# Chunked gated slot attention with a quantised SwiGLU on one core: two transposes taken from TensorE, its loop written out

## The reference

```
n = layernorm(x)
q, k, v, g, s = n@Wq, n@Wk, n@Wv, n@Wg, clip(n@Ws, -32, 32)     # 16 heads; q,k,s 64 wide, v,g 128 wide
z = cumlogsumexp(s, time);  p_t = exp(s_t - z_t);  decay_t = exp(z_(t-1) - z_t)
hk_t = hk_(t-1)*decay_t + k_t (x) p_t ;  ok_t = q_t . hk_t      # 64 slots
w = softmax(ok over slots)
hv_t = hv_(t-1)*decay_t + p_t (x) v_t ;  o_t = w_t . hv_t
x = x + (rmsnorm(o)*g_norm * silu(g)) @ Wo
n = layernorm(x)
x = x + ((silu(n@fp8(gate_w)*gs) * (n@fp8(up_w)*us)) @ fp8(down_w)) * ds
```

## Time and profile before

| | us |
|---|---|
| median of 3 runs | 1432.31 (1431.65 to 1432.43) |
| the profiled execution, whole | 1433.31 |
| its span, first to last instruction | 1431.2 |
| PE busy in the span | 1407.7 (98%) |
| DVE busy | 1001.8 (70%) |
| ACT busy | 430.1 (30%) |
| DMA packets, all queues | 63178, 57.23 MB |

### The profile page before, as it was taken

One profiled execution on the slowest core, in us unless ns is written; L12 is line 12 of the kernel. 1 busy time (PEld: TensorE's weight loads), 2 busy tenths in 40 slices (PEclk: granted clock), 3 DMA queues, 4 the chain that ended last, 5 costly groups with the idle time before them and its releaser, 6 DMA issues.

```text
span 1431.2 us, 23618 instructions
## 1 busy us (share of the span) xinstructions
PE 1407.7 (98%) x8480; PEld 1165.8 (81%) x8480; DVE 1001.8 (70%) x1619; ACT 430.1 (30%) x1243; POOL 144.1 (10%) x106
## 2 busy tenths in 40 slices
PE   7899999999999999999999999999999999999998
PEld 5788888888888888888888888888888878888886
DVE  8677777777777777777777777777777785535354
ACT  4223332333233323332333233323233323222221
POOL 3001110111011101110111011101110010000000
PEclk9999999999999999999999999999999999999999
DMA  6011001100110021002101110111010330000000
GB/s 177 17 56 41 20 26 56 41 19 27 56 41 19 29 61 43 19 27 62 44 19 37 45 41 19 49 40 34 19 54 1 118 118 0 30 0 29 0 30 30
DMA packets 63178, 57.23 MB, mean 40 GB/s; under 512 B 7408, under 2 KB 54256, under 8 KB 63088
## 3 DMA queue, kind: packets, MB, share of 16 engines
q1 hardware_dynamic: 63088, 55.87, 12.8%
HBM read 42.22 MB, written 13.63 MB: 39 GB/s over the span
## 4 chain that ended last, share of the span: by engine, by line
PE 95%; DVE 3%; DMA 1%; issue 0%; SPq 0%; POOL 0%; ACT 0%; DVEq 0%
PE bank L345 18%; PE bank L347 18%; PE bank L346 18%; PE bank L114 12%; PE bank L1384 6%; PE bank L533 4%; PE bank L466 3%; PE bank L516 2%; PE bank L416 2%; PE bank L408 2%; PE bank L455 2%; PE bank L521 1%; PE bank L482 1%; PE bank L438 1%; PE bank L494 1%; PE bank L503 1%
## 5 line engine op out<-in xcount | busy, mean ns | idle before, releaser
L345 PE MATMUL bank<-wvg_hi,xT_hi 128*128 128x512 f32 x512 | 209.0, 408 | 0.6 <-ACT a_and_v L596 0.6
L347 PE MATMUL bank<-wvg_hi,xT_lo 128*128 128x512 f32 x512 | 200.4, 391 | 0.0
L346 PE MATMUL bank<-wvg_lo,xT_hi 128*128 128x512 f32 x512 | 199.9, 390 | 0.0
L596 ACT ACTIVATE a_and_v<-bank 128x256 f32<-128x256 f32 x128 | 49.1, 383 | 296.1 <-PE bank L347 296.0
L954 DVE TENSOR_TENSOR y<-y,bank 128x512 f32<-128x512 f32 x128 | 87.6, 685 | 60.5 <-PE bank L347 60.4
L823 POOL TENSOR_TENSOR rstd<-ssq,neg_half 128x8 f32<-128x8 f32 x32 | 52.4, 1636 | 617.7 <-DVE ssq L925 617.7
L345 PEld LDWEIGHTS bank<-wvg_hi,xT_hi 128*128 128x128 f32 x512 | 96.3, 188 | 22.4 <-ACT a_and_v L596 1.0
L347 PEld LDWEIGHTS bank<-wvg_hi,xT_lo 128*128 128x128 f32 x512 | 96.1, 188 | 21.0
L346 PEld LDWEIGHTS bank<-wvg_lo,xT_hi 128*128 128x128 f32 x512 | 96.5, 188 | 17.3
L873 DVE RECIPROCAL cT<-cT 128x512 f32<-128x512 f32 x32 | 107.3, 3353 | 1.1
L345 PE MATMUL bank<-wo_hi,oT_hi 128*128 128x512 f32 x256 | 106.3, 415 | 0.0
(11 more groups left out here) (157 smaller groups left out, 3194.5 us busy)
## 6 DMA issues: line engine op xcount, KB each, us to landing
fp_weights<-q SPq DMA_DIRECT2D x28, 318.0 KB, 2.7
stage_vg<-in_L_attn_Wv SPq DMA_DIRECT2D x32, 128.0 KB, 2.8
stage_vg<-in_L_attn_Wg SPq DMA_DIRECT2D x32, 128.0 KB, 3.4
stage<-in_L_attn_Wo SPq DMA_DIRECT2D x16, 256.0 KB, 2.6
out<-n_then_result SPq DMA_DIRECT2D x16, 256.0 KB, 2.1
y<-in_L_attn_hidden_states SPq DMA_DIRECT2D x3, 1024.0 KB, 8.7
q<-in_L_ffn_gate_w SPq DMA_DIRECT2D x28, 106.0 KB, 2.0
q<-in_L_ffn_up_w SPq DMA_DIRECT2D x28, 106.0 KB, 2.2
```

The costliest lines, as they stand in the source:

```text
L345: pe.matmul(dst, w_hi, m_hi, start=(k == 0), stop=False)
L346: pe.matmul(dst, w_hi, m_lo, start=False, stop=False)
L347: last = pe.matmul(dst, w_lo, m_hi, start=False, stop=(k == n - 1))
L596: return act.activation(dst, src, ACT.Copy)
```

## The change

- For units 1 to 31 the seven transposes on TensorE and the two copies on ScalarE are gone. VectorE turns 32x32 blocks of `eT` and of the first 3 chunks of `kT` (`e_turn`, `k_turn`) into the tile `o`, which is free at that time. SP stores these in 4 DMAs each (`store_e`, `store_k`) to DRAM with the blocks put in their places, in pieces of 32 floats (128 bytes), and loads each back in 4 DMAs (`load_e`, `load_k`) of 32 partitions each, with rows of 2048 and 1536 bytes. This is done one unit ahead. Unit 0 keeps the transposes.
- TensorE's units 1 to 28 are written out; there is no loop left there in attention.
- `mean_square(u)` moves to the end of unit u, between the last two gates, and `out_norm` stands ahead of `clip`.
- The quantisation has 6 steps: the square, the test against the largest value and two scalings are replaced with one product that overflows and one sum.
- Ahead of unit 0, `sums(0, 0)` (L870, L873) is moved behind the masks of the scores and a gate.

```diff
+BK = 32
+BL = P // BK
-Q8_STEPS = 8
+Q8_STEPS = 6
+    e_blocks = o[:, 0, :, :].rearrange("p c d -> p (c d)")
+    k_blocks = o[:, 1, :, :].rearrange("p c d -> p (c d)")[:, 0:(CH - 1) * P]
...
+        def store_e(nu):
+            sp.wait_ge(s_eb, nu)
+            for i in range(BL):
+                sp.dma_start(e_dram.rearrange("t b (c i m) -> i t (b c) m", i=BL, m=BK)[i],
+                             e_blocks[BK * i:BK * (i + 1), :].rearrange("t (n m) -> t n m", m=BK)
+                             ).then_inc(s_est, 16)
+        def load_e(nu):
+            sp.wait_ge(s_est, 16 * BL * nu)
+            if isinstance(nu, int) and nu == 1:
+                sp.wait_ge(s_hvd, nu)
+            for b in range(BL):
+                sp.dma_start(e_tok[BK * b:BK * (b + 1), :, :].rearrange("t c m -> t (c m)"), e_dram[:, b, :]
+                             ).then_inc(s_eld, 16)
+        def store_k(nu):
+            sp.wait_ge(s_kb, nu)
...
+        def load_k(nu):
+            sp.wait_ge(s_oi, nu)
...
+        store_e(1)
+        load_e(1)
+        store_k(1)
         load_o(0, 1)
+        load_k(1)
         store_q8(0)
         with sp.Fori(0, PAIRS - 1) as h:
             for i in range(1, B + 1):
-                load_q8(h * B + i)
+                u = h * B + i
+                load_q8(u)
                 if i == 1:
                     load_skq(h + 1, 0)
                     load_vg(h + 1)
+                store_e(u + 1)
+                load_e(u + 1)
                 if i == 2:
                     load_skq(h + 1, 1)
+                store_k(u + 1)
+                if i == 2:
                     load_skq(h + 1, 2)
                     load_o(h + 1, 0)
                 if i == B:
                     load_o(h + 1, 1)
+                load_k(u + 1)
                 store_q8(h * B + i)
...
@@ TensorE, unit
-            pe.wait_ge(s_am, 2 * u + 1)
-            for c in range(CH - 1):
-                mm = pe.transpose(T0[:, c * P:(c + 1) * P], kT[:, c * P:(c + 1) * P], ident[:, :])
-            mm.then_inc(s_trk, 1)
-            pe.wait_ge(s_e, u + 1)
-            pe.wait_ge(s_am, 2 * u + 2)
-            for c in range(CH):
-                mm = pe.transpose(T1[:, c * P:(c + 1) * P], eT[par][:, c * P:(c + 1) * P], ident[:, :])
-            mm.then_inc(s_tre, 1)
+            if first:
...
-            if not first:
+            if first:
+                pe.wait_ge(s_ktok, 1)
+                pe.wait_ge(s_etok, 1)
+            else:
+                pe.wait_ge(s_kld, 16 * BL * u)
+                pe.wait_ge(s_eld, 16 * BL * u)
                 pe.wait_ge(s_oev, 2 * u)
...
+            if not first:
+                pe.wait_ge(s_am, 2 * u + 2)
             pe.wait_ge(s_v, (u + 1) * CH)
...
-        with pe.Fori(0, PAIRS - 1) as h:
-            pair_reg[0] = h
-            for i in range(1, B + 1):
-                unit(h * B + i, i)
+        for u in range(1, (PAIRS - 1) * B + 1):
+            unit(u, (u - 1) % B + 1)
@@ ScalarE, head_squares and unit
+            if not a and not last:
+                act.wait_ge(s_est, 16 * BL * (u + 1))
...
-            copy(k_tok.rearrange("p c k -> p (c k)"), T0[:, 0:(CH - 1) * P]).then_inc(s_ktok, 1)
...
-            copy(e_tok[:, :, :].rearrange("p c m -> p (c m)"), T1[:, :]).then_inc(s_etok, 1)
+            if first:
+                act.wait_ge(s_trk, 1)
+                copy(k_tok.rearrange("p c k -> p (c k)"), T0[:, 0:(CH - 1) * P]).then_inc(s_ktok, 1)
+                act.wait_ge(s_tre, 1)
+                copy(e_tok[:, :, :].rearrange("p c m -> p (c m)"), T1[:, :]).then_inc(s_etok, 1)
@@ VectorE
+        def e_turn(nu, ni):
+            dve.wait_ge(s_e, nu + 1)
+            if not (isinstance(nu, int) and nu == 1):
+                dve.wait_ge(s_tro, 2 * (nu - 1))
+            dve.transpose(e_blocks.rearrange("p (b c m) -> p b c m", b=BL, m=BK),
+                          eT[ni % 2][:, :].rearrange("p (c b t) -> p b c t", c=CH, t=BK)).then_inc(s_eb, 1)
+        def k_turn(nu):
+            dve.wait_ge(s_k, nu + 1)
+            dve.transpose(k_blocks.rearrange("p (b c m) -> p b c m", b=BL, m=BK),
+                          kT[:, 0:(CH - 1) * P].rearrange("p (c b t) -> p b c t", c=CH - 1, t=BK)
+                          ).then_inc(s_kb, 1)
...
-                lambda: dve.tensor_tensor(t, w, w, ALU.mult),
-                lambda: dve.tensor_scalar(t, t, FP8_MAX ** 2, FP8_MAX ** 2, ALU.max, ALU.subtract),
-                lambda: dve.tensor_scalar(t, t, HUGE, HUGE, ALU.mult, ALU.mult),
-                lambda: dve.scalar_tensor_tensor(out=w, in0=t, scalar=0.0, in1=w, op0=ALU.mult, op1=ALU.add))
+                lambda: dve.tensor_scalar(t, w, TO_INF, 0.0, ALU.mult, ALU.mult),
+                lambda: dve.tensor_tensor(w, w, t, ALU.add))
...
             if not first:
-                mean_square(u - 1)
-            if not last:
-                clip(nu, ni)
-            if not first:
                 out_norm(u - 1)
+            if not last:
+                clip(nu, ni)
             key_states(u)
             value_states(u)
             if not first:
                 out_lo(u - 1, A)
+            if not last:
+                e_turn(nu, ni)
...
                 add_y(u - 1, i - 1, 0)
                 add_y(u - 1, i - 1, 1)
+            if not last:
+                k_turn(nu)
...
             if not first:
                 dve.wait_ge(s_oi, u)
+            if not last:
+                dve.wait_ge(s_kst, 16 * BL * (u + 1))
             dve.tensor_tensor(wT[:, :], T1[:, :], cT[i % 2][:, :], ALU.mult).then_inc(s_wT, 1)
...
                 gate(2, nu, ni)
+                mean_square(u)
                 gate(3, nu, ni)
...
-        sums(0, 0)
         dve.wait_ge(s_const, 4)
         mask_scores(0, 0)
         gate(B - 1, 0, 0)
+        sums(0, 0)
```

More of the change, by code:

```diff
@@ L309, in store_q8 @@
                          q8[:, :, 0:n]).then_inc(s_fp8_out, 16)
+        def store_e(nu):
[13 more added lines that the diff above has]
+            sp.wait_ge(s_kb, nu)
+            for i in range(BL):
+                sp.dma_start(k_dram.rearrange("t b (c i m) -> i t (b c) m", i=BL, m=BK)[i],
+                             k_blocks[BK * i:BK * (i + 1), :].rearrange("t (n m) -> t n m", m=BK)
+                             ).then_inc(s_kst, 16)
+        def load_k(nu):
+            sp.wait_ge(s_oi, nu)
+            for b in range(BL):
+                sp.dma_start(k_tok[BK * b:BK * (b + 1), :, :].rearrange("t c m -> t (c m)"), k_dram[:, b, :]
+                             ).then_inc(s_kld, 16)
+        ffn.moves = (store_e, load_e, store_k, load_k)
         load_skq(0, 0)
@@ L350, in pair_of @@
         def pair_of(u, i):
-            return u // B if isinstance(u, int) else pair_reg[0] + i // B
-        pair_reg = [None]
+            return u // B
         def wait_drained(j, u):
@@ L383, in job @@
                     pe.wait_ge(s_vgl2, 2 * pair_of(u, i) + 2)
-            if j == ST and (not isinstance(u, int) or u < B):
+            if j == ST and u < B:
                 pe.wait_ge(s_xl, CH * (b + 1))
@@ L401, in scores @@
             pe.wait_ge(s_q, u + 1)
-            if not (isinstance(u, int) and u == 0):
+            if u:
                 pe.wait_ge(s_sub, u)
@@ L429, in unit @@
             nu, ni = u + 1, i + 1
[L431 to L439 removed]
+            if first:
+                pe.wait_ge(s_am, 1)
+                for c in range(CH - 1):
+                    mm = pe.transpose(T0[:, c * P:(c + 1) * P], kT[:, c * P:(c + 1) * P], ident[:, :])
+                mm.then_inc(s_trk, 1)
+                pe.wait_ge(s_e, 1)
+                pe.wait_ge(s_am, 2)
+                for c in range(CH):
+                    mm = pe.transpose(T1[:, c * P:(c + 1) * P], eT[par][:, c * P:(c + 1) * P], ident[:, :])
+                mm.then_inc(s_tre, 1)
             if not last:
@@ L632, in evac @@
             elif j == KTJ:
-                if not first:
-                    act.wait_ge(s_trk, u)
+                if isinstance(u, int) and u == 1:
+                    act.wait_ge(s_trk, 1)
+                elif not first:
+                    act.wait_ge(s_a, u)
+                    act.wait_ge(s_kb, u - 1)
                 copy(kT[:, :], src[:, :]).then_inc(s_k, 1)
@@ L721, in unit @@
                 evac(VG1, nu, ni)
-            head_squares(u, 0)
+            head_squares(u, 0, last)
             if tail and not last:
@@ L726, in unit @@
                 evac(VG2, nu, ni)
-            head_squares(u, 1)
+            head_squares(u, 1, last)
             if not last:
@@ L1326, in _ @@
         load_down(1)
+        store_e, load_e, store_k, load_k = ffn.moves
+        store_e(UNITS - 2)
+        load_e(UNITS - 2)
+        store_k(UNITS - 2)
+        load_k(UNITS - 2)
+        store_e(UNITS - 1)
+        load_e(UNITS - 1)
+        store_k(UNITS - 1)
         sp.wait_ge(w["projected"], JOBS * (UNITS - 1) + STEADY_JOBS.index(QT) + 1)
         load_gate_up(0)
+        load_k(UNITS - 1)
         sp.wait_ge(w["projected"], JOBS * UNITS)
```

33 lines of the change are left out of this document (15 added, 18 removed).

## The result

| | before | after |
|---|---|---|
| median of 6 runs each, us | 1432.37 (1431.63 to 1433.3) | 1409.46 (1407.86 to 1409.88) |
| profiled execution, us | 1433.31 | 1409.40 |
| its span, us | 1431.2 | 1407.3 |

A forecast was written before the change was run, and what follows sets the result against it. PE's instruction stream was taken as the bound (busy 98%). Terms -23.7 - 1.0 - 4.9 + 1.9 + 1.4 = -26.3 took the profiled 1433.3 to 1407.0, a median of 1406.0 us; range 1402 to 1424, 1402 to 1409 without rivals.

The forecast's parts named there:

- The transposes: PE, units 1 to 31: removing seven transposes per unit gains 0.77 us in 29 units, 0.68 in two, 23.7 in all.
- The loop: PE, units 1 to 29: writing out the loop's turns gains 1.0 us (0 to 1.0).
- The start of unit 0: Unit 0: with the sums behind the masks, L455 starts at 47.9 instead of 52.79, gaining 4.9 us.
- rival 3: Unit 0: the clock falls at 44 anyway or its stop lowers it; 3 to 5 us lost; chance 0.15.
- The stop in unit 0: Unit 0, L516: PE stands still waiting on k's store and L1059, losing 1.9 us (0 to 4).
- Wk behind the loads of e: Seven units with i = 2: Wk's later load uses up the exponential's slack before L503; 0.2 us each, 1.4 in all.
- The mark I had set, that ACT must not wait past offset 17: Sign against the forecast: ACT waiting for Wk later than 17 us after its unit begins.
- The price of small pieces: DMA of e and k: 15 ns per 128-byte packet, four stores taking 4.05 us from first issue to last landing.
- rival 1: DMA stores of e and k: small pieces cost as much as 512 bytes, 18 us more, 1424; chance 0.14.
- The mark of 5 us for the stores of e: Sign against the forecast: stores of e taking over 5 us from the first issue.
- Work on DVE: DVE: two new turns per unit at 0.7 us each, against two fewer quantisation passes net; DVE ends even.
- Rival 4: PE: written-out units starve it of instructions; at 0.3 us per unit 8 us are lost, 1414; chance 0.05.

The follow-up runs named there:

- e11_dummy_both: Changed kernel with Wk's load ahead of e's stores (i = 2), unit 0's k store ahead of e's loads, seven unread transposes kept on TensorE: 1426.52 us, ratio 0.9956.
- e3_both: Changed kernel with Wk's load ahead of the stores of e (i = 2) and unit 0's store of k ahead of the loads of e: 1402.84 us, ratio 0.9787.
- e9_best: e3_both plus, in the last unit, TensorE's wait for bank VG3 moved to where the bank is first overwritten: 1402.54 us, ratio 0.9783.
- e4_pe_loop: Changed kernel with TensorE's units 1 to 28 in a loop of 7 turns again: 1411.28 us, ratio 0.9852.
- e6_before_sums: Kernel before with one edit alone, sums(0, 0) moved behind the masks and the gate: 1427.97 us, ratio 0.9966.
- e7_dummy_transposes: Changed kernel with the seven transposes kept on TensorE in units 1 to 31, their results unread: 1438.13 us, ratio 1.0035.
- e12_halves: Changed kernel with each of the four stores of e split into two DMAs of 512 packets of 64 bytes: 1461.64 us, ratio 1.0196.
- e8_eight_steps: Changed kernel with the quantisation in 8 steps again: 1412.91 us, ratio 0.9863.

## Why the prediction was nearly right

The time fell by what the prediction said would give it, PE's stream, and its large terms came out as taken. 1409.46 us is still 0.5 above the 1402 to 1409 that the forecast had for itself; it lies inside the whole range because that made room for rivals. Two small terms were larger than predicted: Wk landed later than its median where no slack was left, and in unit 0 the clock fell behind a stop that had been foreseen.

**The transposes.** Predicted 23.7. Measured 23.65 in the traces (29 x 0.79 + 0.75 + 0) and 23.7 between e11_dummy_both and e3_both. One part was wrong: in unit 31 I took 0.68 off a stretch in which PE only waited for a gate of VectorE behind it; nothing was gained there until e9_best moved the wait. The new wait for the masks cost nothing, as taken.

**The loop.** Predicted 1.0, 1.04 in the traces, 1.8 by e4_pe_loop. The loop does not spare fetches of instructions: 76 packets of 16 KB in e4_pe_loop, 64 in the changed kernel.

**The start of unit 0.** Predicted 4.9, measured 5.17, and shown alone by e6_before_sums, 5.0. The first half of rival 3 fell: standing still for 0.86 us did not lower the clock. The prediction misread one thing here: the fall in the kernel before did not come after more than 2.5 us. PE stopped at 43.11, and the granted clock is 0.99 in 45.0 to 45.4 and 0.50 in 45.4 to 46.0, that is after 2.3 us.

**The stop in unit 0.** Predicted 1.9, lost 3.17. Each time of this step was near: DVE's product ends at 63.4 (predicted 63.2), PE would have started at 61.0 (61.2). What I left to rival 3 happened: behind a stop of 2.42 us the clock fell to 0.50, and this took the rest. The fall does not follow from the length of a stop alone. In the traces of all fourteen kernels PE has 19 stops of 2.0 us or more in attention. Behind 17 of them (2.04 to 4.74 us) the clock fell to 0.50; behind two, 2.33 us in unit 0 of e7_dummy_transposes and 2.70 us in unit 26 of e12_halves, it stayed at 1.00. No stop of 1.57 us or less lowered it. What else decides stays open.

**Wk behind the loads of e.** Predicted 0.2 a unit, 1.4 in all; measured 0.23 to 0.57, 2.75 in all. The step that was mis-sized is the landing: Wk took 2.9 us and not the median of 2.6, and the stores were 0.1 late, and with no slack left each tenth is lost seven times. The mark I had set, that ACT must not wait past offset 17, was passed (17.4), and the error I had allowed for at L503 (0.3) was passed in two units (0.33 and 0.37).

**The price of small pieces.** Right in sum by two errors. Four stores of e take 4.14 us (predicted 4.05), but an issue costs 0.65 and not 0.45, and the landing is 2.2 and not 2.7. The DMA queues of the changed kernel between 532 and 537, in which all stores of e of unit 14 lie (the data of the loads come behind it):

```profile
q1 hardware_dynamic: 2112, 0.26, 30.3%
```

0.303 x 16 x 5 / 2112 = 11.5 ns per packet, where I took 15 and the bounds were 10.6 and 42. So rival 1 fell: a 128-byte piece written to DRAM costs less than half of one of Wk's 512-byte pieces, which are read from it. Per byte it is dearer, 0.090 ns against 0.054. The Trainium skill (DMA: Bandwidth & Descriptors, Specifications) puts the least size for line rate at 512 bytes and says that below it a transfer is done as read-modify-write. The trace agrees that small pieces are slower per byte; that a small piece costs as much as one of 512 bytes, as rival 1 took it, does not show. The mark of 5 us for the stores of e was passed too, in unit 0 (5.03) and in units 20 and 28 (5.07 and 5.16), by fetches early in the stores. What I did not have at all is that the same engines fetch instructions. In the changed kernel seven fetches fall into the time of four units (189.5 to 326.8 us), so the units with i = 4 are hit each time, which have slack, and those with i = 2 never. I take this for luck of the code's length, which no run changes alone; e7_dummy_transposes, with the seven transposes kept in each unit, had other luck and lost 8.9 us more in its units with i = 2.

**Work on DVE.** The turns cost 0.70 and 0.57 (predicted 0.7 each) and DVE's busy time ended even, 1002.6 against 1001.8. That it is free holds only with the six steps: the two more passes in e8_eight_steps cost 3.4 us by the medians and 2.1 in the trace.

L573 did not wait in any unit but unit 0.

**Rival 4** fell: pitches inside and across units are the same 34.26.

The 3.5 us by which the median is above the forecast are 1.35 of Wk and 1.3 of unit 0, less 0.3 at the start, and 1.0 because the execution fell by 23.9 in the profile and by 22.9 in the median. The transposes ended even, since 29 units gave 0.79 instead of 0.77 and unit 31 nothing.

## What to carry to other kernels

Work that leaves the binding engine is worth its full time there, unless it stood in the place of a wait, as in the last unit here. The question is then what the new way makes late. When a store and its load back go through a queue that works in order, ask what stands behind the load: here one weight load and one store in the wrong place cost 6.6 us, and moving them cost nothing. Give each DMA on such a path at least 2 us of slack beyond its median, since in these traces a landing was up to 1.9 us late in a unit whose own work had not changed.

## What was not expected of the hardware

- Four stores to DRAM land up to 1.9 us later when a packet of 16 KB in the instruction queue falls into them (76 of 76 cases); with PE's program as straight code such packets come 19.6 us apart on average.
- The issue of a DMA of 512 pieces of 128 or 64 bytes takes 0.62 us on SP's queue (0.65 with the gap to the next), that of 512 pieces of 512 bytes 0.41.
- A 128-byte packet written to DRAM takes 11.5 ns of a DMA engine.
- Stops of PE of up to 1.57 us left the granted clock at 1.00. Behind 17 of 19 stops of 2.0 us or more it fell to 0.50 (0.50 to 0.67 in the windows shown); behind the other two, 2.33 and 2.70 us, it did not.
